# First batch of an adaptive-linear plus mixture-of-experts kernel: x in two transfers, the first weight chunk in five

## The reference, cut to what matters

```
x: (8, 256, 1024) f32, ids: (8,), weight: (8, 1024, 1024)
w = weight[ids]                               # one 1024x1024 matrix per batch
h = einsum('bsi,boi->bso', x, w)              # the conditional layer
logits = h @ gate_w.T                         # 16 experts, top 2, weights renormalised
moe    = sum over the two experts of silu(g) * u @ w_down[e],  (g, u) = h @ w_gate_up[e]
shared = silu(g_s) * u_s @ shared_w_down,     (g_s, u_s) = h @ shared_w_gate_up
out = x + moe + shared
```

## Time and profile before

| | |
|---|---|
| median of three executions | 1063.52 us |
| the profiled execution, its own time | 1062.65 us |
| its span, first to last instruction | 1060.7 us |
| time around the span | 1.95 us |
| PE busy | 1053.1 us, 99% |
| DVE busy | 634.6 us, 60% |
| ACT busy | 457.7 us, 43% |
| granted TensorE clock, mean | 0.999 |

### The profile page before, as it was taken

How to read it: one execution, slowest core, us unless ns; L and a number is a source line. 1 busy time by engine, 2 the same in 40 slices (tenths; PEclk the granted TensorE clock), 3 DMA queues, 4 the chain that set the end, 5 groups by cost and what they waited for, 6 DMA issues and landing times.

```text
span 1060.7 us, 15852 instructions
## 1 busy us (share of the span) xinstructions
PE 1053.1 (99%) x4817; PEld 870.3 (82%) x4818; DVE 634.6 (60%) x652; ACT 457.7 (43%) x529; POOL 275.6 (26%) x325
## 2 busy tenths in 40 slices
PE   8999999999999999999999999999999999999998
PEld 7888888888888888888888888888888888888887
DVE  5766765636756667876766867353553446544454
ACT  6565644532223556665655755332223222322310
POOL 1000000000036655555555650130003200032040
PEclk9999999999999999999999999999999999999999
DMA  8999877422256779986987865763656336464355
GB/s 330 348 365 350 298 282 266 180 80 80 92 211 208 281 269 343 341 331 241 377 346 261 291 242 205 257 219 119 154 224 238 138 119 188 189 238 146 111 192 204
DMA packets 55782, 248.03 MB, mean 234 GB/s; under 512 B 8194, under 2 KB 21634, under 8 KB 45954
## 3 DMA queue, kind: packets, MB, share of 16 engines
q1 hardware_dynamic: 29826, 161.50, 42.5%
q0 software_dynamic: 19008, 62.41, 16.9%
q10 hardware_dynamic: 6912, 23.66, 5.7%
HBM read 200.87 MB, written 43.52 MB: 230 GB/s over the span
## 4 chain that ended last, share of the span: by engine, by line
PE 99%; DMA 1%; SPq 0%; DVE 0%; issue 0%; ACT 0%
PE bank L588 32%; PE bank L590 32%; PE bank L589 32%; PE bank L613 1%; PE bank L826 1%; DMA raw<-cond_w 1%; PE bank L601 0%; PE bank L759 0%; PE bank L622 0%; DMA ids<-ids 0%; SPq L350 0%; PE bank L746 0%; PE bank L794 0%; DVE w_split_sb L1225 0%; DVE rows L1490 0%
## 5 line engine op out<-in xcount | busy, mean ns | idle before, releaser
L1225 DVE TENSOR_TENSOR w_split_sb<-raw,w_split_sb 128x2048 fp32r<-128x2048 f32 (+3 forms) x154 | 257.5, 1703 | 59.7 <-ACT w_split_sb L912 59.2
L912 ACT ACTIVATE w_split_sb<-raw 128x2048 fp32r<-128x2048 f32 (+3 forms) x154 | 216.0, 1439 | 64.2 <-PE bank L590 53.5
L527 POOL DMA_INDIRECT h_in<-h_dram,idx_h x156 | 176.2, 1130 | 124.0 <-DVE tile_f L1539 80.3
L588 PE MATMUL bank<-hT_hi,w_split_sb 128*128 128x512 f32 x512 | 199.8, 390 | 0.0
L589 PE MATMUL bank<-hT_lo,w_split_sb 128*128 128x512 f32 x512 | 199.3, 389 | 0.0
L590 PE MATMUL bank<-hT_hi,w_split_sb 128*128 128x512 f32 x512 | 199.3, 389 | 0.0
L588 PE MATMUL bank<-w_split_sb,tile_hT 128*128 (+1 forms) x312 | 124.8, 400 | 0.0
L590 PE MATMUL bank<-w_split_sb,tile_hT 128*128 (+1 forms) x312 | 122.0, 391 | 0.0
L589 PE MATMUL bank<-w_split_sb,tile_hT 128*128 (+1 forms) x312 | 121.8, 390 | 0.0
L590 PEld LDWEIGHTS bank<-hT_hi,w_split_sb 128*128 128x128 f32 x512 | 96.2, 188 | 20.0
L589 PEld LDWEIGHTS bank<-hT_lo,w_split_sb 128*128 128x128 f32 x512 | 96.2, 188 | 19.8
(11 more groups left out here) (153 smaller groups left out, 1417.6 us busy)
## 6 DMA issues: line engine op xcount, KB each, us to landing
raw<-sh_gu_w SPq DMA_DIRECT2D x16, 2048.0 KB, 9.1
raw<-exp_gu_w SPq DMA_DIRECT2D x16, 2048.0 KB
raw<-cond_w SPq DMA_DIRECT2D x13, 2048.0 KB, 10.1
y_dram<-y_out ACTq DMA_DIRECT2D x39, 512.0 KB, 4.0
raw<-sh_down_w SPq DMA_DIRECT2D x8, 2048.0 KB, 7.7
raw<-exp_down_w SPq DMA_DIRECT2D x16, 1024.0 KB, 8.4
h_dram<-h_blk POOLq DMA_DIRECT2D x16, 512.0 KB, 9.1
x_raw_sb<-xT SPq DMA_DIRECT2D x7, 1024.0 KB, 9.5
```

What stands on the lines that cost most here:

```text
L527: nc.gpsimd.indirect_dma_start(out=h_in[par][:, i, :], out_offset=None, in_=h_blocks, in_offset=bass.IndirectOffsetOnAxis(ap=idx_h[par][:, ...
L588: nc.tensor.matmul(dst, lhs[0], rhs[0], start=first, stop=False)
L912: return nc.scalar.activation(dst, src, ACT.Copy)
L1225: return nc.vector.tensor_tensor(dst, src, hi.bitcast(F32), ALU.subtract)
```

## The change

x of batch 0 is loaded in two transfers of four k (512 KB, 4 KB per partition) instead of four of two k. ACT issues the first at its start and the second behind its copy of the weights of k 0. The first weight chunk is loaded in five transfers: k 0, k 1, and the pairs k 2-3, k 4-5, k 6-7 (512 KB each) instead of eight single ones. ACT waits for x before the copies of k 0 and of k 4 alone, and for weights before k 0, 1, 2, 4 and 6. The copies, subtractions and matmuls stay as they are, in number, size and order.

```diff
--- before.py
+++ after.py
@@ -65,7 +65,7 @@
     PIECES = 4
     PIECE_K = KT // PIECES
     W_PIECES = 8
-    WPIECE_K = KT // W_PIECES
+    W_FIRST = [(0, 1), (1, 2), (2, 4), (4, 6), (6, 8)]
 
 
     h_dram = nc.dram_tensor("h_dram", [TOKENS, HID], F32).ap()
@@ -172,8 +172,8 @@
         gate_hi_done = sem("gate_hi_done")
         gate_lo_done = sem("gate_lo_done")
 
-        first_x = [sem(f"first_x{i}") for i in range(PIECES)]
-        first_w = [sem(f"first_w{i}") for i in range(W_PIECES)]
+        first_x = [sem(f"first_x{i}") for i in range(2)]
+        first_w = [sem(f"first_w{i}") for i in range(len(W_FIRST))]
 
         second_w = [sem(f"second_w{i}") for i in range(4)]
         third_w = [sem(f"third_w{i}") for i in range(4)]
@@ -344,10 +344,9 @@
 
             def first_loads():
                 a = sp.value_load(small["ids"][0:1, 0:1], min_val=0, max_val=ADAPTERS - 1)
-                for i in range(PIECES):
-                    for k in (2 * i, 2 * i + 1):
-                        c0, c1 = k * WPIECE_K * HALF, (k + 1) * WPIECE_K * HALF
-                        sp.dma_start(raw[0][:, c0:c1], cond_w[bass.ds(a, 1), 0, :, c0:c1].rearrange("o p n -> (o p) n")).then_inc(first_w[k], 16)
+                for i, (k0, k1) in enumerate(W_FIRST):
+                    c0, c1 = k0 * HALF, k1 * HALF
+                    sp.dma_start(raw[0][:, c0:c1], cond_w[bass.ds(a, 1), 0, :, c0:c1].rearrange("o p n -> (o p) n")).then_inc(first_w[i], 16)
                 for i, landed in enumerate(second_w):
                     c0, c1 = i * CH // 4, (i + 1) * CH // 4
                     sp.dma_start(raw[1][:, c0:c1], cond_w[bass.ds(a, 1), 1, :, c0:c1].rearrange("o p n -> (o p) n")).then_inc(landed, 16)
@@ -895,11 +894,10 @@
         @block.scalar
         def _(act):
             def first_x_load(i):
-                act.dma_start(x_raw_sb[:, i * PIECE_K * SEQ:(i + 1) * PIECE_K * SEQ],
-                              xT[0, :, i * PIECE_K * SEQ:(i + 1) * PIECE_K * SEQ]).then_inc(first_x[i], 16)
-
-            for i in range(2):
-                first_x_load(i)
+                x0, x1 = i * KX // 2, (i + 1) * KX // 2
+                act.dma_start(x_raw_sb[:, x0:x1], xT[0, :, x0:x1]).then_inc(first_x[i], 16)
+
+            first_x_load(0)
             act.sem_inc(w_hi, 6)
             act.sem_inc(x_hi, 1)
             act.sem_inc(h_ev, 2)
@@ -927,16 +925,17 @@
 
 
             for i in range(PIECES):
-                act.wait_ge(first_x[i], 16)
+                if i % 2 == 0:
+                    act.wait_ge(first_x[i // 2], 16)
                 k0, k1 = i * PIECE_K, (i + 1) * PIECE_K
                 copy(x_split_sb[0][:, 0, k0:k1, :].rearrange("p k t -> p (k t)"), x_raw_sb[:, k0 * SEQ:k1 * SEQ]).then_inc(first_hi, 1)
-                if i == 0:
-                    first_x_load(2)
                 for k in (2 * i, 2 * i + 1):
-                    act.wait_ge(first_w[k], 16)
+                    for landed, (k0, _) in zip(first_w, W_FIRST):
+                        if k0 == k:
+                            act.wait_ge(landed, 16)
                     copy(w_split_sb[:, 0, 0, k * HALF:(k + 1) * HALF], raw[0][:, k * HALF:(k + 1) * HALF]).then_inc(first_hi, 1)
                     if k == 0:
-                        first_x_load(3)
+                        first_x_load(1)
             act.dma_start(small["gate_raw"][:, :, :], gate_w).then_inc(gate_in, 16)
 
             def gate_hi():
```

## The result

The changed kernel took 1066.36 us in the median of eight executions (1064.35 to 1067.42), beside 1063.27 us for the kernel before (eight executions, 1062.52 to 1063.78): a ratio of 1.0028, 95% interval 1.0019 to 1.0038, so 3.1 us slower. The forecast was 1064.0 us, with 1062.3 to 1065.6 as the range for 8 in 10. The profiled execution took 1064.35 us, the shortest of the eight, with a span of 1062.8 us; it is 1.7 us above the profiled execution of before.

A forecast was written before the change was run, and what follows sets the result against it. PE, busy 1053.1 of 1060.7 us, bounds the kernel. Terms 0 (first half) - 0.9 (k 2) + 1.4 (k 4) = +0.5 us: profiled 1063.15, plus 0.87, median 1064.0 us; 8-in-10 range 1062.3 to 1065.6.

The forecast's parts named there:

- The frame: Whole kernel: time is the start of PE's uninterrupted run plus a constant; copies, subtractions and matmuls sum to zero.
- The first x half: Start-up: it lands at 4.9 us, and any landing before 5.78 costs nothing; term 0.
- The pair k 2-3: Weights of k 2-3 land at 9.9 us and k 2 starts at 11.4, a gain of 0.9 us.
- the landing of half B: Second half of x, issued at 6.4 us, lands at 13.5, between 12.6 and 14.9; k 4 begins at 15.6.
- k 4 late: PE's new wait before k 4, which begins at 15.6 us: +1.4 us in the sum.
- rival (c): Second chunk overtakes half B, which lands at 16.2 us; k 4 starts at 18.3: +3.2 us, 1066.7; chance 0.08.
- a price I left out: PE idle 1.4 to 4 us before k 4: a clock fall was given no price, as no row showed one.
- the 1.95 us around the span: Time of the profiled execution outside its 1060.7 us span, within the 1062.65 us the forecast started from.
- Rival (a): Queues share from issue: half B complete by 12.7 us, k 4 starts by 14.8, kernel 1062.7 us; chance 0.32.
- Rival (b): No change: pair lands at 10.7 us, half B by 13.0, k 2 starts at 12.26; 1063.5 us, chance 0.10.

The follow-up runs named there:

- third piece late: The kernel before, x in four pieces, its third piece issued beside the fourth, behind the copy of k 0's weights: 1066.55 us, ratio 1.0038.
- the halves alone: Kernel before with x in two halves as in the change, weights still in eight single transfers: 1065.79 us, ratio 1.0026.
- the filler: Changed kernel with 32 small matmuls on a constant ahead of the wait for k 4: 1065.28 us, ratio 1.0022; repeated, 1065.37 us, ratio 1.0025.
- the comparison above: Queue packets of the changed kernel (1066.36 us) beside the same kernel issuing its second chunk only after half B landed (1063.49 us).
- the second chunk held: Changed kernel with the second chunk's four transfers issued only after half B of x has landed: 1063.49 us, ratio 1.0007.
- half B early: Changed kernel with half B of x issued behind ACT's first copy of x, near 4.9 us: 1063.03 us, ratio 1.0004.
- the change, again: The changed kernel, unaltered, run a second time, against the kernel before on the same chip: 1067.01 us, ratio 1.0048.
- half B on SP: Changed kernel with half B issued by SP between pairs k 2-3 and k 4-5: 1062.41 us, ratio 0.9994; repeated, 1061.80 us, ratio 0.9991.

## Why the prediction was wrong

The frame held: PE's busy time did not change and, at full clock, the difference lies in when its uninterrupted run begins. The span less the start of k 4 is 1045.6 us in the kernel before (1060.7 - 15.10) and 1045.4 in the first trace of the change (1062.8 - 17.36). The first x half cost nothing: it landed by 4.9 in the first trace and ACT's copy was done long before the weights of k 0 came.

The pair k 2-3: I took a gain of 0.9, measured 0.44 in the first trace. Right in sign, half in size; and it is not steady, since that landing moves more than this from run to run.

The step that failed is the landing of half B. I put it at 13.5, with 14.9 as the far bound, on the argument that x of k 6-7, issued at 6.4, had been served beside the weights issued half a us to a us earlier. I applied that order to the pair k 6-7 and stopped there. The second chunk had moved up to the sixth place of SP's row, and I assumed that place would be held as before. It was not; two transfers of the second chunk were issued ahead of half B or with it, and half B shared the engines with that chunk to the end. It landed at 15.2 and, in the trace with the full loss, at 15.5. The term "k 4 late", +1.4 in the sum, measured 2.70 (17.36 - 11.82 - 2.84). This was rival (c), which I gave 0.08 and priced at +3.2. It came true in its mechanism and, with 2.3 to 2.5 us at k 4, for three quarters of its price, since half B shared with the second chunk and did not wait for all of it. Its condition, that the requests of both queues together held the sixth issue, fits the third piece late: there one request of ACT less by 4.3 us was the only edit, and the hold was gone (333 ns for 1180), with one trace of it. But the second chunk in sixth place is not needed for the loss: the halves alone and the third piece late lose 3.2 and 3.6 us without it, as the weights of k 5 to k 7 go out unheld there. What all three share is that x of k 4 is asked for at 6.7 or later.

The second failure is a price I left out. I wrote that no row shows a fall of the clock and went on without one, though the same text had PE idle for up to 4 us before k 4. It was worth 1.4 us by the matmuls and 1.6 by the filler, in nearly every execution, which took a late k 4 of about 2.5 us to a loss of 3 to 4. The other way went a term that I took as fixed: the 1.95 us around the span became 1.55. With the k 4 of the first trace (+2.26), the clock (+1.4) and this (-0.4) the sum from 1063.5 is 1066.8; measured were 1066.36 and 1067.01.

Rival (a), queues that share from the moment of issue, is refuted by the packets: none of q10 before 10 us in either trace of the comparison above. Rival (b) asked for half B by 13.0, and it came 2.2 us later.

## What to carry to other kernels

In a start-up where every transfer is queued, ask for each piece in the order in which it is needed, counting both queues together; where a merged request takes the place of the later of the two, as half B did, the data of the earlier one is asked for later too, and what stands behind in the other queue can go ahead of it. Before removing requests from a row, see which request now takes the place that used to be held. Removing a request from one engine's queue can do this to the row of the other. Where an edit may leave TensorE idle for longer than before, as here for 2.3 to 2.7 us, put the price of a fall of the clock into the sum, or fill the gap with small matmuls.

## What the hardware showed that I had not expected

- A transfer issued at 6.7 to 7.9 us on ACT's queue had its first packets near 10 us in the changed kernel and with the second chunk held, and in the kernel before with the third piece late (3 packets from 8 to 10 us, 140 from 10 to 12), while one issued at 4.3 moved before 7 in the kernel before. With half B early, issued at 4.93, it had 8 packets from 8 to 9 us and none before; in the second trace of the change, issued at 7.74, none before 11.
- The clock fell after 2.32 and 2.67 us of idle time before k 4 (x halves alone; the change, again) and did not after 2.53 and 2.25 (the first trace of the change; third piece late).
- SP's sixth issue was held for 1.18 to 1.28 us where ACT had issued three transfers by 4.6 us, and took 0.33 to 0.60 where it had issued one or two by 5 us. What holds it, a number of requests or another thing, no run shows.
- With x in halves, one transfer of it issued at the start, the time outside the span is 1.5 to 1.6 us (1064.35 - 1062.8; 1066.58 - 1065.0; 1062.35 - 1060.8), with x in quarters, two issued at the start, 1.9 (1062.65 - 1060.7; 1063.32 - 1061.4; 1063.13 - 1061.2). That 0.35 us is in favour of the halves, part of the gain of half B on SP, and not explained.
